# Beta of the last norm moved from GpSimd to VectorE in a transformer layer with self attention, cross attention and a mixture of experts

## The reference

```python
x = layernorm(x + attn(x, x, x, causal=True), ln1_g, ln1_b)
x = layernorm(x + attn(x, ctx, ctx, causal=False), ln2_g, ln2_b)
x = layernorm(x + moe(x), ln3_g, ln3_b)

def layernorm(x, g, b):
    m = x.mean(-1, keepdims=True)
    v = ((x - m) ** 2).mean(-1, keepdims=True)
    return (x - m) / sqrt(v + 1e-05) * g + b
```

## Time and profile before

| | us |
|---|---|
| runs of the kernel before | 488.32, 482.71, 483.88 |
| their median | 483.88 |
| the profiled execution, its own time | 482.92 |
| its span in the trace | 481.1 |
| the last norm's computing in it | about 457 to 475 |

### The profile page before, as it was taken

The page is one execution under the profiler, slowest core; times in us unless marked ns, Lnnn a source line. Parts: engine busy times, 40 slices in busy tenths (PEclk is TensorE's granted clock), DMA queues, the critical chain, the costliest instruction groups (busy, mean ns, idle before and its releaser), DMA issues.

```text
span 481.1 us, 8890 instructions
## 1 busy us (share of the span) xinstructions
PE 369.3 (77%) x2121; PEld 246.5 (51%) x2121; DVE 305.1 (63%) x1053; ACT 283.8 (59%) x657; POOL 167.1 (35%) x216
## 2 busy tenths in 40 slices
PE   4478599989889989999999988749306999999300
PEld 3235355645545556455555553433205999999300
DVE  6334556777787887787887786473462556565292
ACT  4055379679679678678678678427112555555132
POOL 7322131141431431432432533403130555455353
PEclk9669889999999999999999999966755999999855
DMA  8601232431441351351351350230951122221242
GB/s 223 177 0 34 52 70 53 121 71 40 119 110 40 91 135 38 95 134 27 91 148 24 87 152 2 76 95 28 324 132 44 52 69 68 56 58 53 61 122 87
DMA packets 39370, 41.60 MB, mean 86 GB/s; under 512 B 5018, under 2 KB 32527, under 8 KB 39320
## 3 DMA queue, kind: packets, MB, share of 16 engines
q1 hardware_dynamic: 37048, 36.79, 29.3%
q0 software_dynamic: 2272, 4.24, 2.6%
HBM read 13.66 MB, written 14.79 MB: 59 GB/s over the span
## 4 chain that ended last, share of the span: by engine, by line
PE 48%; DVE 20%; issue 8%; ACT 7%; DMA 6%; POOL 5%; SPq 4%; POOLq 0%; DVEq 0%; ACTq 0%
PE bank L621 8%; PE bank L632 8%; PE bank L539 7%; PE bank L481 4%; PE bank L482 3%; ACT sa_qm L690 3%; PE bank L526 3%; POOL dispatched L1085 3%; DMA sa_km<-sa_ku 3%; DVE ca_nm L820 3%; PE bank L550 2%; PE bank L507 2%; SPq L367 2%; PE bank L506 2%; DVE sa_nm L820 2%
## 5 line engine op out<-in xcount | busy, mean ns | idle before, releaser
L749 ACT ACTIVATE sa_us<-bank,expert_b 128x128 f32<-128x128 f32 x156 | 44.9, 367 | 48.5 <-PE bank L621 48.3
L1062 POOL TENSOR_SCALAR_AFFINE_SELECT sa_pt<-sa_pt 128x512 f32<-128x512 f32 x64 | 39.0, 636 | 62.2 <-ACT sa_pt L698 61.9
L1094 POOL DMA_INDIRECT results<-sa_us,xs x39 | 41.5, 1063 | 51.5 <-DVE sa_us L1005 51.2
L820 DVE TENSOR_REDUCE sa_nm<-bank 128x4 f32<-128x512 f32 x64 | 41.6, 684 | 16.5 <-PE bank L507 16.4
L621 PE MATMUL bank<-xsT,ca_us 128*128 128x128 f32 x312 | 45.1, 290 | 2.5 <-DVE ca_us L993 1.6
L1085 POOL DMA_INDIRECT dispatched<-r_sent,r_row x32 | 31.8, 994 | 43.5 <-DVE r_sent L946 36.1
L690 ACT CAST sa_qm<-bank 8x512 fp32r<-8x512 f32 x64 | 36.8, 576 | 14.9 <-PE bank L514 13.2
L632 PE MATMUL bank<-ca_pt,sa_us 128*128 x312 | 43.7, 283 | 0.1
L690 ACT CAST ca_qm<-bank 8x512 fp32r<-8x512 f32 x64 | 36.8, 575 | 9.5 <-PE bank L514 8.3
L621 PEld LDWEIGHTS bank<-xsT,ca_us 128*128 128x128 f32 x312 | 39.4, 198 | 5.1 <-issue 3.5
L698 ACT ACTIVATE sa_pt<-bank 128x512 f32<-128x512 f32 x64 | 34.8, 596 | 10.1 <-PE bank L526 10.1
(11 more groups left out here) (210 smaller groups left out, 828.7 us busy)
## 6 DMA issues: line engine op xcount, KB each, us to landing
dispatched<-filler SPq DMA_DIRECT2D x17, 520.0 KB, 4.3
sa_km<-sa_ku SPq DMA_DIRECT2D x32, 128.0 KB, 2.4
sa_qm<-sa_qu SPq DMA_DIRECT2D x32, 96.0 KB
ca_qm<-ca_qu SPq DMA_DIRECT2D x32, 96.0 KB
xs<-dispatched SPq DMA_DIRECT2D x39, 65.0 KB, 1.9
ca_km<-ca_ku SPq DMA_DIRECT2D x32, 77.0 KB, 2.1
sa_pt<-in_e_w SPq DMA_DIRECT2D x8, 256.0 KB, 5.0
ca_pt<-in_e_w SPq DMA_DIRECT2D x8, 256.0 KB, 6.1
```

The source lines that it names most:

```text
L749: act.activation(hid[b][:, c, :], bank[2 * b + c // 2][:, P * (c % 2):P * (c % 2) + P], ACT.Gelu, bias=b1[:, bass.ds(expert * FC + c, 1)]) ...
L820: dve.tensor_reduce(k.nm[:, u, g, :], bank[home[k, "scores", u][g % 2]][:, :].rearrange("q (j n) -> q j n", j=J)[:, :, 0:k.keys], AX.X, AL ...
L1062: pool.affine_select(out=blockg, in_=blockg, compare_op=ALU.is_ge, fill=0.0, base=0, pattern=[[0, J], [1, P]], channel_multiplier=-1).then ...
L1094: pool.indirect_dma_start(out=results, out_offset=bass.IndirectOffsetOnAxis(ap=xs[v][:, P:P + 1].bitcast(I32), axis=0), in_=ys[v], in_offs ...
```

## The change

`plus_beta` goes from GpSimd's program to VectorE's, with the same wait (s_g3), the same operands, the same output `o3` and the same increment of s_o3. It is called right behind times_gamma of the same group. GpSimd's loop then has only `deviation`, so its last instruction is the last power. VectorE's order becomes: adds and statistics of 0; of 1, offset(0); of 2, offset(1), gamma(0), beta(0); of 3, offset(2), gamma(1), beta(1); offset(3), gamma(2), beta(2); gamma(3), beta(3).

```diff
--- before.py
+++ after.py
@@ -1031,6 +1031,11 @@
                 dve.wait_ge(s_xn3, TN * (q + 1))
                 dve.tensor_tensor(y3[:, t, :], y3[:, t, :], g3[:, :].rearrange("q (o d) -> q o d", o=1).to_broadcast([P, TN, D]), ALU.mult).then_inc(s_g3, 1)
 
+            def plus_beta(q):
+                t = slice(TN * q, TN * q + TN)
+                dve.wait_ge(s_g3, q + 1)
+                dve.tensor_tensor(o3[:, t, :], y3[:, t, :], beta3[:, :].rearrange("q (o d) -> q o d", o=1).to_broadcast([P, TN, D]), ALU.add).then_inc(s_o3, TN)
+
             for q in range(TAIL + 2):
                 if q < TAIL:
                     add_and_measure(q)
@@ -1038,6 +1043,7 @@
                     offset(q - 1)
                 if q >= 2:
                     times_gamma(q - 2)
+                    plus_beta(q - 2)
 
         @block.gpsimd
         def _(pool):
@@ -1100,16 +1106,8 @@
                 t = slice(TN * q, TN * q + TN)
                 pool.tensor_tensor(rs3[:, t], ba3[:, t, 1], half[:, :].to_broadcast([P, TN]), ALU.pow).then_inc(s_rs3, 1)
 
-            def plus_beta(q):
-                t = slice(TN * q, TN * q + TN)
-                pool.wait_ge(s_g3, q + 1)
-                pool.tensor_tensor(o3[:, t, :], y3[:, t, :], beta3[:, :].rearrange("q (o d) -> q o d", o=1).to_broadcast([P, TN, D]), ALU.add).then_inc(s_o3, TN)
-
-            for q in range(TAIL + 2):
-                if q < TAIL:
-                    deviation(q)
-                if q >= 2:
-                    plus_beta(q - 2)
+            for q in range(TAIL):
+                deviation(q)
 
 
 # ---- launch: one core; inputs and outputs as the reference has them ----
```

## The result

The changed kernel takes 477.86 us in the median of 20 runs, the kernel before 482.81 (20 runs beside them). The ratio is 0.9916, 95% interval 0.9895 to 0.9937: 4.1 us faster (3.0 to 5.1), where the prediction had 1.15; its forecast was 482.3 us, with a range from 480.7 to 484.7. The ratio compares only executions in the faster of two states that this kernel shows, so it isn't quite that of the two medians (0.990). The profiled execution took 477.56 us.

A forecast was written before the change was run, and what follows sets the result against it. Bound: the last norm's chain of waits, mostly on VectorE, with GpSimd on it twice at the end. Terms 0.72 - 1.03 - 0.16 - 0.67 = -1.14 (walk -1.15); 483.4 - 1.15 = 482.3 us, range 480.7 to 484.7.

The forecast's parts named there:

- 8: Stores at the end: each starts with its beta's end; the last lands 1.15 us earlier, the 3.9 us behind it stay.
- Rival D: Span's end: it hangs on something other than the last store, so no gain, 483.4 us; chance 3%.
- Step 1: Last norm, VectorE: beta(0) enters the queue ahead of group 3's adds and delays them by 0.72 us.
- Steps 3 and 4: Last power takes 1.43 us, hiding beta(1); offset(3), without GpSimd's beta beside it, takes 0.12 instead of 1.15: -1.03.
- Rivals A and B: Last norm: port contention with the power halves the gain, 482.9 us, 10%; offset's 1.15 has another cause, 483.3 us, 8%.
- Steps 5 to 7: Norm's end: gamma(2), beta(2) cost nothing; gamma(3) 0.68 instead of 0.84, -0.16; beta(3) on VectorE, -0.67.
- Rival C: Last norm: VectorE's longer program needs one more code load, 2.2 us of standing still, +1.05, 484.5 us; chance 4%.

The follow-up runs named there:

- e5: Changed kernel plus one GpSimd 128x512 add with beta right behind the last power, its result unneeded; offset(3) took 1.15 us, span 476.4 us.
- e6: Changed kernel plus one GpSimd 128x512 memset, which only writes, right behind the last power; offset(3) took 0.16 us, span 481.3 us.
- e2: Changed kernel plus only a wait for all betas behind GpSimd's last power, no memset; span 484.5 us, single run 486.2 us.
- e1: Changed kernel plus a wait for all betas and a 128x1 memset behind GpSimd's last power; median 482.31 us, ratio 0.9995 to the kernel before.

## Why the prediction was wrong

- **The step that failed is 8, its last sentence: "The last lands 1.15 earlier, and the 3.9 us from there to the span's end stay."** Counted from the norm's first add, the last landing came 0.80 earlier, and the 3.9 us didn't stay. They were not a fixed end of the program behind the last landing; they were the rest of GpSimd's closing, 6.17 us from beta(3)'s end, of which 2.3 passed while the last store was on its way. On the same count GpSimd's end moved from 17.85 to 13.59, so the closing now runs beside ScalarE, gamma, beta and the store, and the stretch from the last beta to the span's end falls from 6.17 to 2.63: 3.54 us that the sum had put at nothing.
- Rival D had the right place: "the end hanging on something other than the last store", with the 3.9 us as its sign. Its sign (a last store earlier and a span that isn't) didn't come, and its price was wrong. I took it as a reason for no gain, though the change moves GpSimd's end too, further than any other.
- Step 1 (+0.72): the table gives +0.95 up to the last aggregate. Beta(0) starts 0.79 behind gamma(0), not 0.72, and group 3's first add comes 0.80 later behind gamma(0); another 0.20 is no part of the change: group 1's first add waited for its load (2.92 behind group 0's instead of 2.72). Some hundredths in other rows make up the rest.
- Steps 3 and 4 were right: power 1.42, offset 0.16 (1.03 forecast to go, 0.99 gone). That GpSimd's add was the cause is shown by e5 and e6. Rivals A and B fell: beta(1) took 0.69 within the power, and the power ended 0.87 behind gamma(1)'s end.
- Steps 5 to 7: gamma(3) 0.69 as forecast, beta(3) ends 1.48 behind gamma(3)'s start where I had 1.41, again the 0.79 between two dependent operations. From the last aggregate to the last beta 1.75 went, where the steps had 1.87.
- Rival C did not come: no idle piece of VectorE stands in the tail that is put down to issue.
- The mechanisms seen inside the norm were right in sign and within 0.35 us in sum (0.80 for 1.15; without the late load, 1.00). The sum left out a term of 3.54 us. The prediction also held that about 1% (4.8 us) is the least that a measurement of this kernel can tell; the interval of 3.0 to 5.1 us around 4.1 shows that 20 runs of each tell less.

## What to carry to other kernels

When the chain of waits ends and the span still has microseconds left with nothing running, that stretch belongs to something: measure it from each engine's last instruction, in two kernels if possible, before calling it fixed. If GpSimd has issued many DMAs, let its program end early: here 71 of them cost about 6.1 us at the end, hidden if GpSimd's last instruction comes that long before the span's end. And where a short VectorE operation with two SBUF inputs takes some ten times its usual time and ends with an operation of GpSimd's, suspect that operation, and test it as e5 does, by putting one like it there.

## What the runs showed of the hardware

- Behind GpSimd's last instruction the program needed 0.33 us with no DMA of its own, 0.42 with one, 3.28 with 36, 6.15 with 71 and 2.66 with 142, with every one of them long landed (small kernels, one run each), and 6.08 to 6.17 with 71 in the large kernel; behind ScalarE's late copy at most 0.3.
- In the run with 142, GpSimd stood 2.8 us longer than usual between the 113th DMA and the 114th, and the closing fits the 29 behind that stop. Shown in one run only.
- A wait at the end of GpSimd's program is enough to put that closing off (the span ends 6.31 us behind the last beta in e2, 6.33 with a memset in e1, and 2.63 in the changed kernel).
- A GpSimd add of 128x512 that reads SBUF held VectorE's 128x4 two-input operation for 1.15 us instead of 0.12 to 0.17; a GpSimd memset of the same tile did not. The 128x4 power (1.42 us), which reads SBUF too, held no add of VectorE's: beta(1), wholly beside it, took its 0.69.
